# The convolution of a Mamba stage: three shifted taps taken from TensorE and put on VectorE

## The reference, cut to what matters

```
xz = x @ in_proj_w + in_proj_b ; xc, z = split(xz)
xc = silu(conv(xc) + conv_b)          # depthwise, taps at t-3, t-2, t-1, t
delta_s, B, u = split(xc @ x_proj_w + x_proj_b)
delta = softplus(delta_s @ dt_proj_w + dt_proj_b)
h[t] = exp(-delta*(n+1)) * h[t-1] + delta*B*u    # n = 0..15 ; y = sum over n of h
out = ((y + u*D) * silu(z)) @ out_proj_w + out_proj_b
```

## Time and profile before

| | |
|---|---|
| time, median of 3 runs | 3438.0 us (3434.74 to 3440.54) |
| the profiled execution, its own time | 3436.78 us |
| its span in the profile | 3434.7 us |
| busy over the span: TensorE, VectorE, ScalarE, GpSimd | 88%, 71%, 51%, 65% |
| the Mamba stage | from the start to about 1770 us |
| two turns of the loop | 215.0 us |

### The profile page before, as it was taken

One profiled execution on the slowest core, in us unless ns is written; L12 is line 12 of the kernel. 1 busy time (PEld: TensorE's weight loads), 2 busy tenths in 40 slices (PEclk: granted clock), 3 DMA queues, 4 the chain that ended last, 5 costly groups with the idle time before them and its releaser, 6 DMA issues. The chain is left out here.

```text
span 3434.7 us, 54203 instructions
## 1 busy us (share of the span) xinstructions
PE 3009.1 (88%) x17168; PEld 2332.1 (68%) x17184; DVE 2425.9 (71%) x3701; ACT 1763.7 (51%) x3332; POOL 2235.8 (65%) x1403
## 2 busy tenths in 40 slices
PE   6899989999899998999857999896888876898988
PEld 2565655556555565556547889896767766898988
DVE  2888888888888888888855666664566654666674
ACT  3666666656666566665534444442333333444443
POOL 3878978888788887888855555562233335555554
PEclk9999999999999999999978999998999997999999
DMA  4321221112211122111144434342112214343442
GB/s 127 105 96 40 76 77 64 51 39 76 77 62 52 40 76 77 63 52 40 70 155 125 121 86 112 96 110 38 54 60 63 70 57 129 86 109 98 99 109 46
DMA packets 184203, 273.14 MB, mean 80 GB/s; under 512 B 35686, under 2 KB 156171, under 8 KB 175813
## 3 DMA queue, kind: packets, MB, share of 16 engines
q1 hardware_dynamic: 148676, 227.92, 20.5%
q0 software_dynamic: 35328, 42.76, 7.1%
HBM read 188.89 MB, written 94.72 MB: 83 GB/s over the span
## 5 line engine op out<-in xcount | busy, mean ns | idle before, releaser
L599 POOL TENSOR_TENSOR dbu<-du,bb 128x1024 f32<-128x1024 f32 x512 | 1199.1, 2360 | 153.5 <-DVE hs L738 148.7
L738 DVE TENSOR_TENSOR_SCAN hs<-da,dbu 128x1024 f32<-128x1024 f32 x512 | 1150.8, 2279 | 103.7 <-ACT da L686 36.3
L686 ACT ACTIVATE da<-delta 128x512 f32<-128x512 f32 x1024 | 570.2, 595 | 292.1 <-DVE hs L738 277.2
L838 PEld LDWEIGHTS yT<-ident,hs 128*128 128x128 f32 x4096 | 483.4, 146 | 168.0 <-issue 133.6
L838 PE MATMUL yT<-ident,hs 128*128 128x128 f32 x4096 | 540.6, 281 | 22.0 <-DVE hs L738 22.0
L1306 POOL TENSOR_TENSOR ffn_w_lo<-ffn_w,ffn_w_hi 128x512 fp32r<-128x512 f32 x256 | 373.8, 1479 | 132.1 <-ACT ffn_w_hi L1301 131.5
L1382 PE MATMUL ffn_ybank<-ffn_w_hi,ffn_hT_hi 128*128 128x256 f32 x1280 | 392.2, 306 | 74.2 <-DVE ffn_hT_lo L1370 74.2
L1383 PE MATMUL ffn_ybank<-ffn_w_lo,ffn_hT_hi 128*128 128x256 f32 x1280 | 378.0, 295 | 0.0
L1384 PE MATMUL ffn_ybank<-ffn_w_hi,ffn_hT_lo 128*128 128x256 f32 x1280 | 377.4, 295 | 0.0
L1352 PE MATMUL ffn_hbank<-ffn_rowsT_hi,ffn_w_hi 128*128 128x320 f32 x1024 | 321.8, 314 | 24.7 <-ACT ffn_h L1363 22.5
L1382 PEld LDWEIGHTS ffn_ybank<-ffn_w_hi,ffn_hT_hi 128*128 128x128 f32 x1280 | 260.9, 204 | 90.0 <-DVE ffn_hT_lo L1370 90.0
(11 more groups left out here) (233 smaller groups left out, 5243.3 us busy)
## 6 DMA issues: line engine op xcount, KB each, us to landing
bb<-b_rows SPq DMA_DIRECT2D x64, 1024.0 KB, 4.6
ffn_w<-L_ffn_W SPq DMA_DIRECT2D x64, 1024.0 KB, 10.1
slots<-empty SPq DMA_DIRECT2D x40, 530.0 KB, 6.7
ffn_rows<-slots SPq DMA_DIRECT2D x32, 662.5 KB, 5.1
xt<-L_attn_a_x SPq DMA_DIRECT2D x16, 512.0 KB, 3.9
x<-L_attn_a_x SPq DMA_DIRECT2D x16, 512.0 KB, 3.9
x_after_mamba<-x SPq DMA_DIRECT2D x16, 512.0 KB, 3.0
a_x<-x_after_mamba SPq DMA_DIRECT2D x16, 512.0 KB, 5.0
```

The lines of the kernel that those rows point to most:

```text
L599: pool.tensor_tensor(dbu[:, s % DEEP], du[:, dt, :].unsqueeze(1).to_broadcast([P, SN, T]), bb[:, q * SN:(q + 1) * SN, :], ALU.mult).then_i ...
L686: ins = act.activation(da[:, s % 2, i, :], delta[:, par, dt, :], ACT.Exp, scale=-float(q * SN + i + 1))
L738: dve.tensor_tensor_scan(flat[0], flat[1], flat[2], 0.0, ALU.mult, ALU.add).then_inc(scanned.sem, 1)
L838: mm = pe.matmul(yT[:, j * P:(j + 1) * P], hs[:, s % DEEP, i, j * P:(j + 1) * P], k.ident[:], start=False, stop=(q == QS - 1 and i == SN - ...
```

## The change

Of the convolution, the bank now holds the running sum. `conv_input` writes the last tap (scale and bias) back into the bank in place of the tile `last_tap`; the new `conv_step` on VectorE adds the three shifted taps into the bank, each one waiting for the one before; `tanh_x` waits for the third. `conv_taps`, `w_diag`, `last_tap` and the 12 instructions that build the diagonals are gone. The orders of the ring and most positions ("at s ==") on all engines are new.

```diff
-        b_tap, w_diag = sb("b_tap", [P, ND]), sb("w_diag", [P, ND, DC - 1, P])
+        b_tap = sb("b_tap", [P, ND])
...
             act.activation(xc[:, m, DC - 1:], bank, ACT.Identity, bias=b_in[:, m:m + 1])
-            if has_first(turn - 1) or m >= 2:
-                act.wait_ge(conv_mm.sem, conv_mm.at(turn, m - 1))
-            act.activation(last_tap[:, m % 2, :], bank, ACT.Identity, bias=b_tap[:, m:m + 1],
+            act.activation(bank, bank, ACT.Identity, bias=b_tap[:, m:m + 1],
                            scale=w_conv[:, m, DC - 1:DC]).then_inc(conv_in.sem, 1)
...
-            act.wait_ge(conv_mm.sem, conv_mm.at(turn, m + 1))
+            act.wait_ge(conv.sem, conv.at(turn, (DC - 1) * (m + 1)))
...
+        def conv_step(dve, turn, m):
+
+            bank = bank_of(f"I{m}")
+            dve.wait_ge(conv_in.sem, conv_in.at(turn, m + 1))
+            for tap in range(DC - 1):
+                if tap > 0:
+                    dve.wait_ge(conv.sem, conv.at(turn, (DC - 1) * m + tap))
+                dve.scalar_tensor_tensor(bank, xc[:, m, tap:tap + T], w_conv[:, m, tap:tap + 1], bank,
+                                         ALU.mult, ALU.add).then_inc(conv.sem, 1)
...
-        def conv_taps(pe, turn, m):
-
-            bank = bank_of(f"I{m}")
-            pe.wait_ge(conv_in.sem, conv_in.at(turn, m + 1))
-            for tap in range(DC - 1):
-                pe.matmul(bank, w_diag[:, m, tap, :], xc[:, m, tap:tap + T], start=(tap == 0), stop=False)
-            mm = pe.matmul(bank, k.ident[:], last_tap[:, m % 2, :], start=False, stop=True)
-            mm.then_inc(conv_mm.sem, 1)
...
-RING_JOBS = ("G3", "Z0", "O0", "U2", "T0", "T1", "U3", "I0", "I1", "G0", "O1", "Z1", "I2", "I3", "RT0", "S", "DA0",
-             "DA1", "RT1", "DA2", "DA3", "G1", "RL", "U0", "Z2", "U1", "G2", "RP", "Z3", "-")
+RING_JOBS = ("G3", "Z0", "U2", "T0", "O0", "T1", "U3", "I0", "I1", "O1", "G0", "I2", "Z1", "I3", "RT0", "S", "DA0",
+             "DA1", "DA2", "G1", "DA3", "RT1", "RL", "U0", "Z2", "U1", "RP", "G2", "Z3", "-")
...
-                for m in range(ND):
-                    for tap in range(DC - 1):
-                        dve.tensor_scalar(w_diag[:, m, tap, :], k.ident[:], w_conv[:, m, tap:tap + 1], None,
-                                          ALU.mult).then_inc(diag_ready, 1)
```

More of the change, by code:

```diff
@@ L472, in mamba_phase @@
         xc = sb("xc", [P, ND, DC - 1 + T])
[L473 removed]
+        hx, th = sb("hx", [P, ND, T]), sb("th", [P, 2, T])
         db = sb("db", [48, T])
@@ L1030, in one_turn @@
                         if s == 22 and first:
-                            step_size(act, turn, par, 1)
+                            step_size(act, turn, par, 2)
+                            step_size(act, turn, par, 3)
+                        if s == 23 and first:
                             exp_part(act, turn, 0)
-                        if s == 22 and late:
+                        if s == 23 and late:
                             route_turned(act, turn, 1)
                         if s == 24 and first:
-                            step_size(act, turn, par, 2)
-                            step_size(act, turn, par, 3)
@@ L1038, in one_turn @@
                             exp_part(act, turn, 1)
                             log_part(act, turn)
-                        if s == 25 and first:
+                        if s == 26 and main:
+                            summed_copy(act, turn, row, 2)
+                        if s == 26 and late:
+                            route_exp(act, r, turn - 2)
+                        if s == 27 and main:
+                            gate_input(act, turn, 2)
+                        if s == 29 and first:
@@ L1041, in one_turn @@
                             skip_input(act, turn, turn, 0)
-                        if s == 26 and has_first(turn + 1):
+                        if s == 29 and has_first(turn + 1):
                             prompt_apply(act, norm, xt, xt, turn + 1)
[L1044 to L1049, removed]
@@ L1079, in one_turn @@
                             silu_z(dve, turn, 3)
+                        if s == 1 and late:
                             gate(dve, turn, 3)
@@ L1083, in one_turn @@
                             step_input(dve, turn, row, 1 - par, 2)
-                        if s == 3 and late:
+                        if s == 5 and late:
                             residual(dve, turn, turn - 2, 0)
-                        if s == 7 and main:
+                        if s == 6 and main:
                             step_input(dve, turn, row, 1 - par, 3)
-                        if s == 10 and first:
+                        if s == 7 and has_first(turn + 1):
+                            dve.wait_ge(x_ld.sem, x_ld.at(turn + 1, 16))
+                            prompt_stats(dve, norm, xt, turn + 1)
+                        if s == 8 and first:
+                            conv_step(dve, turn, 0)
+                        if s == 9 and first:
+                            conv_step(dve, turn, 1)
+                        if s == 11 and first:
                             silu_x(dve, turn, 0)
-                        if s == 11 and first:
-                            silu_x(dve, turn, 1)
+                        if s == 12 and late:
+                            residual(dve, turn, turn - 2, 1)
                         if s == 12 and is_turn(turn, 0):
@@ L1094, in one_turn @@
                             dve.tensor_tensor(b_skip[:], b_u[:], d_skip[:], ALU.mult).then_inc(skip_ready, 1)
-                        if s == 13 and main:
+                        if s == 13 and first:
+                            silu_x(dve, turn, 1)
+                        if s == 14 and main:
                             gate(dve, turn, 0)
-                        if s == 13 and late:
-                            residual(dve, turn, turn - 2, 1)
+                        if s == 14 and late:
                             route_stats(dve, turn, turn - 2)
-                        if s == 15 and main:
+                        if s == 15 and first:
+                            conv_step(dve, turn, 2)
+                        if s == 16 and main:
                             silu_z(dve, turn, 1)
@@ L1140, in one_turn @@
                             in_proj(pe, turn, 1 - par, "Z0", ND + 0)
-                        if s == 0 and late:
-                            out_proj(pe, turn, 0)
-                        if s == 0 and main:
                             x_proj(pe, turn, 2, 0)
@@ L1147, in one_turn @@
                             turn_x(pe, turn, 0)
-                        if s == 1 and late:
+                        if s == 2 and late:
+                            out_proj(pe, turn, 0)
+                        if s == 3 and first:
+                            turn_x(pe, turn, 1)
+                        if s == 3 and late:
                             out_proj(pe, turn, 1)
-                        if s == 2 and first:
-                            turn_x(pe, turn, 1)
-                        if s == 2 and main:
+                        if s == 3 and main:
@@ L1194, in one_turn @@
+                        if s == 19 and first:
                             dt_proj(pe, turn, 3)
```

129 lines of the change are left out of this document (57 added, 72 removed).

## The result

The changed kernel takes 3537.4 us (median; 3530.0 to 3541.2) against 3439.3 us of the kernel before beside it: ratio 1.0285, 95% interval 1.0265 to 1.0305, or 98 us more. The forecast was 3450 us, the top of its range 3500.

A forecast was written before the change was run, and what follows sets the result against it. TensorE was taken as the fullest engine (99.7 of 107.5 us a turn), VectorE as the bound after. Fifteen turns at +1.1 us give +16, the start -4: +12 us on 3438.0, forecast 3450 us, range 3386 to 3500.

The forecast's parts named there:

- VectorE took over: Loop: TensorE falls to about 86 us of 107.5 a turn and VectorE becomes the bound; 3450 us, chance 0.42.
- the direction leaned to slower: Whole kernel: chance 0.47 of slower, 0.38 of faster by over 0.2%, 0.15 of within 0.2%.
- The taps: Twelve added VectorE instructions a turn: 2.3 us a block, 9.3 us a turn, bounds 6.8 to 10.8.
- ScalarE's in-place write: Last tap written into the bank instead of SBUF: same price as before, 776 ns.
- The clock went below 0.94: Sign expected in the profile after: TensorE's granted clock at 0.94 or less.
- VectorE must spend 94.1 + 9.3 = 103.4 us, so only 4.1 us of waits may stay: VectorE, per turn: its 94.1 us without waits plus 9.3 of taps leaves 4.1 of waits for 107.5 us.
- 108.6: Forecast time of a turn in us: 94.1 + 9.3 + 5.2 - 0.7 + 0.7, or +1.1.
- waits that stay: VectorE, per turn: 5.2 us, from the turn's head (2.0), tanh of block 3 (0.7) and the chain to `step_input` 0 (2.5).
- the 0.7 of the clock: TensorE's lower clock level adds 0.7 us a turn, an estimate between nothing and 3.6.
- the rival: TensorE's I2, Z1, I3 and small projection run at the lower clock: 3 us a turn over forecast, 3495 us, chance 0.22.
- the prediction's own reckoning: Lower-clock time from the mean clock: (1 - 0.96) x 215 / 0.5 = 17 us in two turns of the kernel before.
- The start: Start and turn 0: 2.44 us of diagonals go and turn 0's convolutions save 2 us, together -4 us.

The follow-up runs named there:

- table of two by two: Kernel before, diagonal products kept or gone, VectorE taps absent or present: 1 and 1.0438 with products, 0.9953 and 1.0254 without.
- a_ports: Changed kernel with the token copy as a `tensor_reduce` and the two statistics instructions on GpSimd: 1.0273 of the kernel before.
- a_warm: Changed kernel plus zero-matrix products on TensorE (4 ahead of a turn's first sum, 2, 3 and 4 behind sums of steps 9, 11, 14): 1.0148.
- a_ports_warm: Changed kernel with copy as `tensor_reduce`, statistics instructions on GpSimd, plus zero-matrix products on TensorE: 1.0161 of the kernel before.
- b_taps: Kernel before with all four blocks' taps on VectorE at steps 9, 10, 15 and 16, other positions unchanged: 1.0254.
- b_both: Kernel before with the diagonal products kept on TensorE and VectorE passing over each bank three times by a factor of zero: 1.0438.
- b_ports: Kernel before, as a control, with the token copy as a `tensor_reduce` and the two statistics instructions on GpSimd: 1.0011.
- b_warm: Kernel before with 3 zero-matrix products on TensorE ahead of the first sum of each turn: 1.0043.
- b_notaps: Kernel before with the diagonal products gone and no taps on VectorE, the three shifted taps left out of the convolution: 0.9953.
- the four at 228.7 us: Changed kernel, it with the copy replaced, with copy and statistics instructions replaced, and the latter with taps back on TensorE: two turns 228.4 to 228.9 us.
- b_tap0: Kernel before with only block 0's three taps on VectorE, at step 9: 0.9951.
- b_tap3: Kernel before with only block 3's three taps on VectorE, at step 16: 1.0106.
- three blocks: Kernel before with the taps of blocks 0, 1 and 2 on VectorE and `route_apply` moved ahead of `tanh_x` 2: 1.0145.
- a_apply: Changed kernel with `route_apply` on ScalarE moved from behind the tanh of block 2 to ahead of block 3's eviction: 1.0398.
- b_stats7: Kernel before with only `prompt_stats` moved, from step 16 to step 7: 1.0100.
- a_copy: Changed kernel with only the token copy made a `tensor_reduce`: 1.0311 of the kernel before.
- b_taps_warm: Kernel before with all four blocks' taps on VectorE plus 16 zero-matrix products a turn on TensorE: 1.0444.

## Why the prediction was wrong

**Right.** TensorE ceased to be the fullest engine, VectorE took over, and the direction leaned to slower. The taps cost 2.31 us for three, starts about 0.78 apart, 9.0 us busy a turn against 9.3. ScalarE's in-place write cost no more: its busy time in two turns fell from 137.96 to 137.43 us. The clock went below 0.94.

**The step that failed: "VectorE must spend 94.1 + 9.3 = 103.4 us, so only 4.1 us of waits may stay".** This is a balance over a whole turn. It lets the taps fill 8.2 of the 13.4 us of waits, wherever those stand. By it the taps would cost 9.3 - 8.2 = 1.1 us a turn. The table of two by two shows what they really meet on the old layout: steps in which VectorE has hardly a wait, so that they cost 9.3 us a turn beside the products and 6.2 without them, and TensorE's relief alone buys 0.4. Four engines that are coupled within two to four steps don't average over 32 of them.

**Terms that were mis-sized in the new layout.** After, a turn is 114.35 us: 103.3 busy, 7.6 of waits for others, 3.5 of the loop's start and small gaps. The forecast had 108.6. The 5.8 us are 2.4 more waits that stay (7.6 against 5.2) and two stalls behind GpSimd, L175's (5.6 - 0.3) / 2 = 2.6 us and the copy's (4.7 - 0.3) / 2 = 2.2. That is 7.2; against it stand the 0.7 of the clock, which the measured waits hold already, 0.3 of the taps (9.0 against 9.3) and small overlaps. The stalls had no term in the sum, and the small moves were counted as free: `prompt_stats` moved alone costs 1.0%. But this split closes only the books. a_ports took out 2.7 us of it and the turn stayed, so what is taken out of VectorE's list comes back as waits elsewhere.

**The clock** was given 0.7 us a turn, with 3 more in the rival. a_warm gave back 1.4% or 47 us, 3.1 a turn, and a_ports_warm beside a_ports 1.1% or 39 us, 2.6 a turn: on this layout the fill was worth about what the rival gave the clock. Its path was another: in the turn shown above only I2 ran at the lower level (3.59 us at 800.71); Z1 and I3 behind it took 3.60 together, 1.8 each. The rival asked for waits over about 3.85 us; here waits of 3.02 and 3.15 us have the lower level behind them too. TensorE was forecast near 172 us busy in two turns and is at 183; by the prediction's own reckoning, an estimate, it spends (1 - 0.92) x 228.7 / 0.5 = 37 us at the lower level in place of 17. As the cause of the whole loss the clock fell: on the old layout the fill made b_taps slower, and b_both at 0.940 is slower than b_taps at 0.919. The Trainium skill ("TensorE: Matmul & The Clock Gate", section "Part 4: PE-mode transpose") says that transposes don't count as work for the clock in the same way. TensorE's transposes at half speed at 783 and 814 us don't bear that out, since a wait of 3.02 and of 4.42 us stands ahead of them; the earlier trace rows speak against it, and no run here had transposes alone as its difference.

**The start** was given -4 us. The diagonals' 2.4 us did go (the norm's statistics end at 15.4 in place of 17.9 us), but the first scan starts at 74.8 us in place of 73.5. On the way there the gain was lost again; in b_taps, with the old positions, the first scan starts at 70.2.

**Open.** Why the same kind of fill helps the new layout and harms the old one isn't settled. In the old it restores just the amount of TensorE's work that was taken away (1.0444 beside b_both's 1.0438), some of it behind step 18, in a stretch where TensorE is full (830 to 856 us: 25.99 of 26); in the new it stands mostly in TensorE's waits. How the 2.5% of the new layout alone divide over its moves wasn't tried beyond `prompt_stats`. And many of these kernels share the time of two turns: besides the four at 228.7 us, before, b_ports and b_warm run mostly at 215.0 to 215.3, and b_notaps goes back and forth between 211.7 and 215.0. With b_tap0 at 211.8, b_tap3 at 218.4, three blocks at 221.8 and a_apply at 235.5, the loop's time seems to settle on values some 1.7 us a turn apart, though b_taps, b_stats7 and a_warm lie between them. So an edit may take work out and win nothing, or lose a whole step for little, and part of what is put down to waits above may be that. What sets these values no run tests.

## What to carry to other kernels

Before work is moved from the fuller engine to the emptier one, read both engines' busy time in the very steps where it goes: a whole turn's idle time is no room. Move it block by block, and measure each: block 0 of four gained 0.5%, block 3 lost 1.1%, all four lost 2.5%. In a list laid out by hand, a small instruction's place against GpSimd's is part of its price.

## What the hardware showed that was not expected

- A stall on the ports between VectorE and GpSimd stands in the profile as busy time of a tiny instruction, not as a wait: 170 ns became 2818 (median of 16), and the group's mean in the list is the only sign. Taken from one instruction it moved to a later one with two SBUF inputs: to the first in a_copy (154 ns to 2.22 us), past that one to L368 in a_ports (208 ns to 2.31 us). The taps, with one input from SBUF and one from the bank, took 723 to 757 ns in all 192 cases.
- Work without use made the kernel faster: 13 products with zeros a turn on TensorE took the ratio from 1.0285 to 1.0148, with the granted clock from 0.92 to 0.98 in the loop. On the old layout such products cost time each time (b_warm, b_taps_warm).
- Taking all 13.8 us a turn of diagonal products off the fullest engine, with nothing in their place, was worth 0.5%, and 0.4 us a turn from the first scan on; the granted clock fell from 0.95 to 0.92 in the loop.
